# Half of attention's products with V in the next batch's turn, weights in 32 pieces, 12 unread products per turn

## The reference, cut to what matters

```python
Wqk = jnp.einsum('hij,hkj->hik', tril, tril)
t = jnp.einsum('bshd,hde->bshe', xh, Wqk)
scores = jnp.einsum('bshe,bthe->bhst', t, xh) / jnp.sqrt(jnp.asarray(d, x.dtype))
attn = jax.nn.softmax(scores, axis=-1)
Vh = (x @ Wv.T + bv).reshape(bs, seq_len, H, d)
out = jnp.einsum('bhst,bthd->bshd', attn, Vh).reshape(bs, seq_len, emb_dim)
return out @ Wo.T + bo
```

## Time and profile before

| | us |
|---|---|
| runs shown, median (lowest, highest) | 1570.67 (1566.55, 1570.69) |
| the profiled execution, its own time | 1579.64 |
| its span, first to last instruction | 1577.9 |

### The profile page before, as it was taken

One profiled execution on the slowest core, in us unless ns is written; L12 is line 12 of the kernel. 1 busy time (PEld: TensorE's weight loads), 2 busy tenths in 40 slices (PEclk: granted clock), 3 DMA queues, 4 the chain that ended last, 5 costly groups with the idle time before them and its releaser, 6 DMA issues. The chain is left out here.

```text
span 1577.9 us, 31368 instructions
## 1 busy us (share of the span) xinstructions
PE 1088.8 (69%) x9744; PEld 779.6 (49%) x9744; DVE 1086.1 (69%) x2356; ACT 681.2 (43%) x1360; POOL 456.6 (29%) x607
## 2 busy tenths in 40 slices
PE   4515887774299997675767868266488786469991
PEld 2212232224288883453545745144376665458881
DVE  3867999997555555547967754888667776746653
ACT  4505555553265453114426622244266655234440
POOL 0051777772254545610001100000033333222203
PEclk9557999995599998887968977688556766579996
DMA  6600000001345544202000000000012222112213
GB/s 198 206 4 11 0 1 0 1 1 48 94 123 137 159 129 144 79 29 80 1 0 1 1 1 0 0 1 0 28 58 105 82 82 82 48 40 67 62 52 117
DMA packets 45459, 89.64 MB, mean 57 GB/s; under 512 B 8096, under 2 KB 34373, under 8 KB 42437
## 3 DMA queue, kind: packets, MB, share of 16 engines
q1 hardware_dynamic: 38274, 67.97, 13.7%
q0 software_dynamic: 6912, 18.88, 4.3%
q10 hardware_dynamic: 144, 1.05, 0.2%
HBM read 71.84 MB, written 16.04 MB: 56 GB/s over the span
## 5 line engine op out<-in xcount | busy, mean ns | idle before, releaser
L909 POOL TENSOR_TENSOR scan_ch<-scan_hs,scan_ct 128x452 f32<-128x452 f32 x128 | 143.4, 1141 | 81.4 <-DVE scan_hs L1019 67.3
L932 PE MATMUL scan_py<-scan_ch,ident 128*128 128x452 f32 x256 | 130.8, 600 | 41.1 <-POOL scan_ch L909 31.0
L1019 DVE TENSOR_TENSOR_SCAN scan_hs<-scan_abar,scan_bx 128x452 f32<-128x452 f32 x128 | 132.9, 1079 | 0.8 <-ACT scan_abar L981 0.5
L2620 POOL TENSOR_TENSOR mha_prob_lo<-mha_prob,mha_prob_hi 113x452 f16<-113x452 f32 x64 | 65.3, 1042 | 135.2 <-ACT mha_prob_hi L2781 135.2
L458 PE MATMUL m0x_ph<-m0x_xb,m_w_hi 128*128 128x128 f16 x456 | 100.0, 221 | 0.7 <-ACT m0x_xb L1625 0.5
L459 PE MATMUL m0x_ph<-m0x_xb,m_w_hi 128*128 128x128 f16 x456 | 100.0, 221 | 0.0
L460 PE MATMUL m0x_ph<-m0x_xb,m_w_lo 128*128 128x128 f16 x456 | 99.6, 220 | 0.0
L1690 DVE TENSOR_SCALAR m3x_a<-m3x_ph,m3x_b 128x128 f32<-128x128 f32 x184 | 49.7, 344 | 69.2 <-ACT m3x_ah L1651 67.3
L932 PEld LDWEIGHTS scan_py<-scan_ch,ident 128*128 128x128 f32 x256 | 40.5, 192 | 112.4 <-POOL scan_ch L909 104.6
L981 ACT ACTIVATE scan_abar<-ssm_dt,ssm_a 128x448 f32<-128x448 f32 x128 | 80.8, 638 | 23.7 <-DVE scan_hs L1019 22.1
L1687 DVE SCALAR_TENSOR_TENSOR m0x_a<-m0x_ph,m0x_b,m0x_gate 128x128 f32<-128x128 f32 x114 | 34.7, 347 | 72.1 <-issue 36.3
(11 more groups left out here) (675 smaller groups left out, 3888.1 us busy)
## 6 DMA issues: line engine op xcount, KB each, us to landing
mha_wbuf<-m3w SPq DMA_DIRECT2D x16, 1024.0 KB, 4.8
tok_wbuf<-m0w SPq DMA_DIRECT2D x15, 768.0 KB, 5.5
m0x_b<-m0b SPq DMA_DIRECT2D x57, 128.0 KB
m_out<-m0x_yo SPq DMA_DIRECT2D x57, 128.0 KB
m3x_b<-m3b SPq DMA_DIRECT2D x23, 128.0 KB, 3.0
m_out<-m3x_yo SPq DMA_DIRECT2D x23, 128.0 KB
m_rows<-m0r_parts SPq DMA_DIRECT2D x4, 448.0 KB
m_rows<-m3r_parts SPq DMA_DIRECT2D x4, 448.0 KB
```

What stands on the lines that cost most here:

```text
L909: pool.tensor_tensor(ch[r][:], hs[r][:], ct[n % 2][:], ALU.mult).then_inc(weighed, 1)
L932: pe.matmul(py[c][:, 0:GT], core.ident[:], ch[u % R][:], start=n == 0, stop=n == NS - 1).then_inc(summed, 1)
L1019: dve.tensor_tensor_scan(hs[u % R][:], abar[c][:, 0:GT], bx[u % R][:], 0.0, ALU.mult, ALU.add).then_inc(scanned, 1)
L2620: pool.tensor_tensor(prob_lo[g][:], prob[g % 2][:], prob_hi[g][:], ALU.subtract).then_inc(p_low, 1)
```

## The change

- On PE weigh_v(j-1, 2) and weigh_v(j-1, 3) are made in turn j, behind second_pass(j, 0); project_u(j+2) and project_v(j+1) with first_pass(j+1, 2) stand ahead of weigh_v(j, 0); turn_peaks(j+1) stands ahead of project_out(j-1). At the end of the turn keep_warm(j, 12) makes 12 products of 452 columns into s2[0], which nothing reads.
- On DVE the order becomes low of the last turn's second piece, maxima 0 and 1, normalize, split_v, maxima 2 and 3, repeat_peaks, split_o, split_peaks, split_u, low, add. On ACT take_q moves up, one high stands between take_o and take_qm, round_prob 2 and 3 and a second high behind take_qm.
- Weights come in 32 pieces of 128x1024 (512 KB) over 3 buffers, two pieces a turn, instead of 16 of 128x2048 over one.
- project_v waits for add two batches back; take_v waits for it in its place.

The core of the diff:

```diff
+class CutWeights(MoeWeights):
+    CUTS = 2
...
+    def load(self, sp, n):
+        whole, cut = divmod(n, self.CUTS)
+        need(sp, self.lo_done[n % self.depth], n // self.depth)
+        sp.dma_start(self.buf[n % self.depth][:], self.d[self.m.name + "w"][:, whole, cut * self.cols:(cut + 1) * self.cols]
+                     ).then_inc(self.landed[n % self.depth], 16)
...
-        mw = MoeWeights(st, m, d, 1)
+        mw = CutWeights(st, m, d, 3)
...
                 def project_v(j):
                     need(pe, v_out, j)
-                    need(pe, h_added, j - 1)
+                    need(pe, h_added, j - 2)
...
+                def keep_warm(j, n):
+                    need(pe, exped, j * 4 + 4)
+                    for _ in range(n):
+                        pe.matmul(s2[0][:, 0:452], core.xt_hi[:, 0, 0:L], core.xt_hi[:, 1, 0:452], start=True, stop=True)
...
                     if now:
                         second_pass(j, p, 0)
+                    if behind:
+                        weigh_v(j - 1, 1 - p, 2)
+                        weigh_v(j - 1, 1 - p, 3)
                     if ahead1:
                         first_pass(j + 1, 1 - p, 0)
+                    if ahead2:
+                        project_u(j + 2)
                     if now:
                         second_pass(j, p, 2)
+                    if ahead1:
+                        project_v(j + 1)
+                        first_pass(j + 1, 1 - p, 2)
                     if now:
                         weigh_v(j, p, 0)
                         weigh_v(j, p, 1)
+                    if ahead1:
+                        turn_peaks(j + 1)
                     if behind:
                         project_out(j - 1)
                     if ahead1:
-                        first_pass(j + 1, 1 - p, 2)
...
+                        keep_warm(j, 12)
...
                 def take_v(j):
                     act.wait_ge(v_ready, j + 1)
+                    need(act, h_added, j - 1)
                     need(act, pv_done, j * 4)
```

More of the change, by code:

```diff
@@ L1110, in __init__, with small_tiles @@
                                                   for w in (m.w1_hi, m.w1_lo, m.w2_hi, m.w2_lo))
+        self.small_tiles(st)
+    def small_tiles(self, st):
+        m = self.m
         if m.mult:
@@ L1172, in low, with __init__, place, high @@
         ins.then_inc(self.lo_done[b], 1)
+class CutWeights(MoeWeights):
+    CUTS = 2
+    def __init__(self, st, m, d, depth):
+        self.m, self.d, self.depth = m, d, depth
+        self.cols = KC * m.NF * 128 // self.CUTS
+        self.buf = [st.sb(f"wbuf{p}", [128, self.cols]) for p in range(depth)]
+        self.landed, self.lo_done = ([st.sem(f"w_{n}{p}") for p in range(depth)] for n in ("landed", "lo"))
+        self.hi_done = st.sem("w_hi")
+        self.small, self.ready = st.sem("small_landed"), st.sem("mult_ready")
+        self.w1h, self.w1l, self.w2h, self.w2l = (w[:].rearrange("p e k n -> p e (k n)")
+                                                  for w in (m.w1_hi, m.w1_lo, m.w2_hi, m.w2_lo))
+        self.small_tiles(st)
+        self.pieces = m.E * 2 * self.CUTS
+    def place(self, n, w1, w2):
+        whole, cut = divmod(n, self.CUTS)
+        expert, half = divmod(whole, 2)
+        return (w1, w2)[half][:, expert, cut * self.cols:(cut + 1) * self.cols]
+    def load(self, sp, n):
+        whole, cut = divmod(n, self.CUTS)
+        need(sp, self.lo_done[n % self.depth], n // self.depth)
+        sp.dma_start(self.buf[n % self.depth][:], self.d[self.m.name + "w"][:, whole, cut * self.cols:(cut + 1) * self.cols]
+                     ).then_inc(self.landed[n % self.depth], 16)
+    def high(self, act, n):
+        act.wait_ge(self.landed[n % self.depth], n // self.depth * 16 + 16)
+        act.activation(self.place(n, self.w1h, self.w2h), self.buf[n % self.depth][:], ACT.Copy,
+                       scale=WS).then_inc(self.hi_done, 1)
+    def low(self, eng, n):
+        eng.wait_ge(self.hi_done, n + 1)
+        eng.scalar_tensor_tensor(self.place(n, self.w1l, self.w2l), self.buf[n % self.depth][:], WS,
+                                 self.place(n, self.w1h, self.w2h), ALU.mult,
+                                 ALU.subtract).then_inc(self.lo_done[n % self.depth], 1)
 def stage_route(nc, core, m):
@@ L2586, in stage_attention @@
         v_high, p_high, p_low = st.sem("v_high"), st.sem("p_high"), st.sem("p_low")
-        mw = MoeWeights(st, m, d, 1)
-        assert m.steps == NB
+        mw = CutWeights(st, m, d, 3)
+        assert mw.pieces == 2 * NB
         (ones_set, u_ready, q_ready, ac_ready, v_ready, v_out, s1_ready, maxed, peaks_ready, mt_ready,
@@ L2607, in _ @@
                 mw.load_small(sp)
-                steps(sp, m.steps, lambda at: mw.load(sp, at))
+                for n in range(mw.pieces):
+                    mw.load(sp, n)
             @block.gpsimd
@@ L2798, in turn @@
                         round_prob(j, 0)
-                        round_prob(j, 1)
-                        if isinstance(j, int) and j == 0:
+                        if j == 0:
                             act.wait_ge(ones_set, 4)
                         take_v(j)
+                        round_prob(j, 1)
+                    if ahead2:
+                        take_q(j + 2)
+                    if now:
+                        exponential(j, 2)
+                        exponential(j, 3)
                     if behind:
@@ L2805, in turn @@
                     if now:
-                        exponential(j, 2)
-                        exponential(j, 3)
+                        if j == 0:
+                            act.wait_ge(mw.ready, 2)
+                        mw.high(act, 2 * j)
+                    if ahead1:
+                        take_qm(j + 1)
+                    if now:
                         round_prob(j, 2)
                         round_prob(j, 3)
[L2810 to L2816, removed]
+                        mw.high(act, 2 * j + 1)
                 turns(act, prologue, turn)
@@ L2885, in turn @@
                     if behind:
+                        mw.low(dve, 2 * j - 1)
+                    if ahead1:
+                        maxima(j + 1, 1 - p, 0)
+                        maxima(j + 1, 1 - p, 1)
+                    if behind:
                         normalize(j - 1)
@@ L2889, in turn @@
                     if ahead1:
[L2890 to L2896, removed]
                         maxima(j + 1, 1 - p, 2)
@@ L2899, in turn @@
                         repeat_peaks(j + 1, 1 - p)
+                    if behind:
+                        split_o(j - 1)
+                    if ahead1:
+                        split_peaks(j + 1, 1 - p)
                     if ahead2:
                         split_u(j + 2, p)
-                    if ahead1:
-                        split_peaks(j + 1, 1 - p)
                     if now:
-                        mw.low(dve, at)
+                        mw.low(dve, 2 * j)
+                    if behind:
+                        add(j - 1)
                 turns(dve, prologue, turn)
```

## The result

The changed kernel takes 1609.53 us (median of 4 runs, 1608.99 to 1611.81), the kernel before 1570.68 beside it: 2.6% slower, ratio 1.0257 with a 95% interval of 1.0237 to 1.0276, or +38.9 us. Forecast were 1615 and "slower".

The account below looks back on a forecast made before the run. The prediction took a loop of waits between DVE and PE, with PE's clock, as the bound: 15 turns going from 12.16 to 15.2 us give +45.6, less 1.1 at the end, on 1570.67: 1615 us, range 1567 to 1632.

Parts of the forecast that it names:

- (a): PE from the start of second_pass(j, 0): second_pass, weigh_v, first_pass with hand-over, 1.9 us at 2.4 GHz.
- (b): DVE: maxima 0 and 1 (1.20 us), then normalize to the end of split_v (2.33), together 3.5 us.
- (c): PE: project_v and first_pass to its last result, DVE waiting; 1.9 us at 2.4 GHz, 3.1 at 1.2.
- (d): DVE: maxima 2 and 3 with repeat_peaks 1.43 us, then split_o 0.3, together 1.7 us.
- (e): PE: project_out 1.11 us and 12 unread products 2.3, together 3.4 at 2.4 GHz, before the next second_pass.
- the loop itself: Attention turn alternating between PE and DVE waits: 12.4 us at 2.4 GHz, 17.9 at 1.2, 15.2 expected.
- where the clock falls and rises: PE's clock: falls shortly before or in project_v after a gap over 2 us, rises in the middle of the 12 products.
- The end: Stage's end: one half of low on the path instead of the whole, -1.1 us once.
- The base: Stage's +44.5 us added to the median of the runs shown, 1570.67 us, not the profiled 1579.64, giving 1615.
- That the clock stays up: Rival: PE at 2.4 GHz all through, since 12 products lift the turn's activity; +2.5 us, 1573; chance 0.08.
- the lower bound is VectorE: Rival: clock up, products hidden behind the wait for am, VectorE bounds at 11.3 us a turn; 1557; chance 0.11.
- The clock hardly rises: Rival: PE's clock hardly rises in the products or falls again at once; 17.5 us a turn, 1650; chance 0.08.

Follow-up runs that it names:

- the version with 6: Changed kernel with split_v ahead of normalize on VectorE and 6 unread products a turn in place of 12: 1544.97 us, 0.9844 of the kernel before.

## Why the prediction was right

The steps, in the turn from 1264.56 to 1279.14 and in the longer one behind it:

| step | forecast, us | short turn | long turn |
|---|---|---|---|
| (a) second_pass, weigh_v, first_pass | 1.9 at 2.4 GHz | 2.04 | 2.04 |
| (b) maxima, normalize, split_v | 3.5 | 3.46 | 3.46 |
| (c) project_v, first_pass | 1.9, or 3.1 at 1.2 GHz | 1.84 | 2.52 |
| (d) maxima, repeat_peaks, split_o | 1.7 | 1.79 | 1.79 |
| (e) project_out | 1.95 at 1.2 GHz | 2.06 | 2.06 |
| (e) 12 products | 3.4, half of them slow | 3.39 | 4.28 |
| sum | 15.2 | 14.58 | 16.15 |

Right were the loop itself, all signs on DVE and PE that the prediction named (a wait ahead of the second maxima of 1.90 and 2.58, none ahead of add, 2.01 ahead of project_v, second_pass directly behind the products), and, in the short turns, where the clock falls and rises. The exchange that decides it: the wait of 2.23 for project_out went, and waits for first_pass came, 67.6 us in the stage; and the products stand where PE waits for nobody.

**Mis-sized: (c) at 1.2 GHz.** 2.52 and not 3.1. I added project_v (1.95) and first_pass (1.02) end to end; in the trace the first score product starts 1.46 us behind project_v's first, beside the first bias product, and not behind the last:

```profile
1286.10 0.46 PE L2688 MATMUL mha_pvo<-mha_bv_hi,ones 1*113 1x256 f16 x1
1286.10 0.34 PE L2701 MATMUL mha_s<-mha_same 32*113 32x113 f16 x2
```

**Mis-sized: the products in the long turns**, 4.28 for 3.4. There the clock was at 0.50 until 1294, 0.60 in the microsecond behind it and 1.00 from 1295 on, so nearly all twelve ran at 1.2 GHz. The two misses and the short turns' (c) at 2.4 GHz nearly cancel. What is left cancels too: the two kinds of turn average 15.37, and the first turn, which I counted like the rest, took 12.87, since it has neither project_out nor normalize; that makes 15.21. To hit 15.2 was right by the loop, and by luck in its last tenths. That the turns alternate was not foreseen. It follows two courses of the clock in the rows (low for about 7 us in one turn and 10 in the next); what sets which of them comes is open.

**The end** gave 16.33 - 15.84 = 0.5 us and not 1.1. The low is off the path there, as forecast, but the last normalize now waits for the second half of weigh_v, which the change put into this last turn, and that for GpSimd, whose two subtractions took 3.59 us where they took 2.04 before:

```profile
1363.59 3.59 POOL L2666 TENSOR_TENSOR mha_prob_lo<-mha_prob,mha_prob_hi 113x452 f16<-113x452 f32 x2 [2.41 <-ACT mha_prob_hi L2835]
1367.96 1.57 DVE L2914 RECIPROCAL mha_rec<-mha_pacc 128x226 f32<-128x226 f32 x1 [1.67 <-PE mha_pacc L2747]
```

**The base.** For the stage I said +44.5, and it was +45.2. The medians differ by 38.9. The 6 us between, by which 1615 missed 1609.53, are not explained. They lie in the stages that the change does not touch, if the stage took in the other executions what it took in the two traced ones; no trace shows that.

**The rivals.** That the clock stays up came true only with split_v ahead of normalize, in most turns. That the lower bound is VectorE was right as a bound, 10.18 a turn in place of my 11.3, for I had counted the wait of 1.9 in (c) as one that stays. "The clock hardly rises" is what the version without products shows, for its whole length. For the rule of the Trainium skill that the prediction weighed ("TensorE: Matmul & The Clock Gate", section "HAM oscillation — how this bites in real kernels"), that keeping the engine at work avoids the throttling: the changed kernel was throttled anew in every turn with the 12 products in it, and in only four of them with the same 12 once the gap on the other side was short; six were then enough for a run of turns. So far rule and runs agree once both gaps of the loop are counted. The version with split_v early and no products does not fit it: TensorE was busy for 158 of 170 us, its waits were 1.1 us at most, and it had 1.2 GHz throughout. There the measurement decides: to keep the engine at work was not enough.

## To carry to other kernels

Filler work meant to hold a clock lost 1.2% here while a gap of 2 us stood elsewhere in the loop, and gained 0.9% once that gap was gone: shorten the longest gap first, and only then try filler, with as little as still holds the level (here 8 or 6 in place of 12, worth another 0.5 to 0.8%). When an instruction moves on one engine, look at what stands ahead of its partner on the other engine: here 2 us of normalize ahead of a split of 0.4 us cost more than all that the change could gain. Count a loop by its semaphores and compare us a turn; for the changed kernel it repeated to 0.01 us where whole times differed by half a per cent.

## What the runs showed of the hardware

**GpSimd and VectorE hold each other up.** The two halves of low are the same work, but the second took 1.73 us for 1.22 in each of the turns shown, and GpSimd's two subtractions beside them 3.05, where the pair that no low stands beside takes 2.04:

```profile
1266.96 2.04 POOL L2666 TENSOR_TENSOR mha_prob_lo<-mha_prob,mha_prob_hi 113x452 f16<-113x452 f32 x2 [4.54 <-ACT mha_prob_hi L2835]
1274.77 3.05 POOL L2666 TENSOR_TENSOR mha_prob_lo<-mha_prob,mha_prob_hi 113x452 f16<-113x452 f32 x2 [5.77 <-ACT mha_prob_hi L2835]
```

The times fit turns taken, not sharing. GpSimd's first subtraction ends near 1275.8 (half of 2.04 behind 1274.77); the first low runs to 1276.9 at its normal length; the second subtraction ends at 1277.82, 0.9 behind that; the second low, started at 1277.17, ends at 1278.90, 1.08 behind GpSimd. The Trainium skill, "SBUF — State Buffer", section "Who interferes with whom", says that VectorE and GpSimd share a pair of ports as an exclusive lock, and that a VectorE instruction with two SBUF inputs contends with a GpSimd instruction that reads SBUF; both kinds are that here, and the trace agrees. The version with the pieces alone is the counterpart: no low there lies beside a subtraction, GpSimd's pairs take 2.04 us throughout, and two lows, one behind the other, take 2.35:

```profile
1256.00 2.35 DVE L1215 SCALAR_TENSOR_TENSOR m_w_lo<-mha_wbuf,m_w_hi 128x1024 f16<-128x1024 f32 x2
```

No run changed this alone. It cost nothing in the steady turns of the changed kernel, where both lie beside the products. At the stage's end it stands on the path (the 3.59 above), and in the version with products in the gap PE's wait of 1.57 us for the low part ends at 1252.82, right behind subtractions that took 3.05 from 1249.72. In the version with 6 the late low stands directly ahead of the maxima on the engine that is the bound (1241.90 and 1243.63 above), 0.5 us a turn that another place might give back; it was not tried.

**The clock without wide products.** In two versions TensorE was busy for 148 and 158 of 170 us, mostly with products of 113 and 256 columns, and its clock stayed at 1.2 GHz throughout, while some turns of before reach 2.4 GHz with the same products in another order. In the version with six products of 452 columns a turn the clock was at 2.4 GHz for over ten turns, with TensorE busy for 89 of 106 us, a smaller share than in either. Busy time as the profile counts it does not tell which level will be granted.
